# Second attention of a two-layer transformer kernel: VectorE instead of ScalarE copies the transposed probabilities out of PSUM bank 5

## The chip, the cores and the metric

The kernel runs on one core of a Trainium2 chip. The metric is the device time of one execution in microseconds; lower is better. Engines are named as in the profile: PE is TensorE (PEld its weight loads), DVE is VectorE, ACT is ScalarE, POOL is GpSimd, SP is SyncE, which issues most DMAs.

## The reference

The input x has 16 sequences of 128 tokens with 256 features, all in float32. Two blocks run one after the other, and x is added to the result.

- Block 1: a conditioned layer norm, self-attention with 16 heads of 128, an output projection, and a feed-forward network with 1024 hidden units and Gelu.
- Block 2: an RMS norm; queries for 16 heads and keys and values for 4 heads (each is shared by 4 query heads); RMS norm and rotary embedding of queries and keys; causal attention; an output projection; then a router that sends each token to 2 of 8 experts.

The part that matters here is the attention of block 2:

```python
q = rmsnorm(q, q_norm_w); k = rmsnorm(k, k_norm_w)      # then rotary embedding
k = jnp.repeat(k, n_rep, axis=1); v = jnp.repeat(v, n_rep, axis=1)
scores = jnp.einsum('bhqd,bhkd->bhqk', q, k) * scale
scores = jnp.where(causal[None, None], scores, jnp.finfo(scores.dtype).min)
attn = jnp.einsum('bhqk,bhkd->bhqd', jax.nn.softmax(scores, axis=-1), v)
hidden = hidden + attn @ o_w.T
```

## The kernel before, in words

The program is written by hand: each engine has its own instruction stream, in order, and waits on semaphores with fixed counts. No scheduler moves anything. The 16 sequences are handled in 4 groups of 4. The order of the stages is the first attention (to about 600 us), the first feed-forward network, the second attention (the stage of this change, about 650 to 1105 us), and the experts.

**The second attention** is a pipeline of steps. `attention2(step, expert)` calls an engine's `step(s)` for u = 0 to 15 in each group g = 0 to 3, and after the last group for u = 16 to 22: the drain, in which no new queries come in and from u = 19 on the first expert tiles are worked on too. One step brings in one key/value head of one sequence with its 4 query heads, so every tile is 128 x 512. `s.kv` is u mod 4. A step with kv = 0 also makes the keys and values of a new sequence (`new_seq`), one with kv = 1 scales and transposes the keys. `s.live(k)` is true where the work item that came in k steps ago is to be handled. An item goes through the steps like this:

- u: PE makes the queries in bank 0 (L1949). DVE multiplies them with the rotary tables into qr and rb (L1508, L1512), POOL adds the two (L642), ACT squares them into sq (L903), DVE sums that into q_ms (L1587), and POOL makes rq, the factor of the norm (L654, L658).
- u + 1: PE transposes qr into bank 4 (L2063), ACT copies it to q_t (L915).
- u + 2: PE makes mask and scores in bank 3 (L2093, L2096), once the exps of the item before have left the bank.
- u + 3: DVE takes the negative maximum nmax of bank 3 (L1550) and multiplies it to nb (L1554). ACT makes four exps into p2 (L889), each with a read of its accumulator. DVE makes rinv (L1576), POOL multiplies p2 by it (L646).
- u + 4: PE transposes p2 into bank 5 (L2071). **The copy of this change** takes bank 5 to the tile pt2 (L922 on ACT, shown in the profile as pt).
- u + 5: PE multiplies pt2 with the values into bank 6 (L2032), ACT rounds it into o2_hi (L910), DVE makes the remainder o2_lo (L1591).
- u + 6: PE multiplies both with the output weights into bank 7 (L2006), twelve matmuls. After the fourth head DVE adds bank 7 to xres (L1596), at kv = 1.

**The order within a step.** PE: keys, queries, output product (waits for o2_lo), values, weighted values (wait for pt2), transposes of qr and p2, keys' transposes, mask and scores (wait for the exps). At u = 12 the weighted values come before the values product, at u = 0 both products come before the keys. ACT: exps, key squares, sq, o2_hi, q_t, router logits (u = 11), **pt2**, v2 (kv = 0), k_t (kv = 1), weight pieces. DVE: nmax, nb, norm statistics (u = 7), key rotation, key scaling (kv = 1), query rotation, rinv, key and query sums, o2_lo, xres add (kv = 1), and then what only some steps have: norm_rows (L1032, u = 9), its transposed copies (L1040, u = 10), the routing parts (u = 11 to 14), placing of rows (`place_rows`, u = 15 and, for g of 2 and more, u = 0), the tables of the expert tiles (`first_tiles`, u = 16 and 18), and the remainders of weight pieces (L1639 for u = 5 to 12 of group 0, wd_lo in L1644 for u = 17 to 19), each after ACT has rounded its piece (L940, L948). POOL also scatters the token rows by indirect DMA (`send`, L614), the last eight at u = 16 to 18; SP loads the first expert tile when all of these have landed.

The semaphore that the copy counts up is g_ph. PE waits for it ahead of the weighted values and ahead of the next transposes into bank 5; the first expert tiles wait for its last count. g_tp counts the transposes, g_pvp the weighted values.

Of the kernel before, what the change touches and what calls it, by code (L numbers as in the profile page):

```python
# [24 lines left out]
ACT = mybir.ActivationFunctionType  # L25
# [28 lines left out]
def program(nc, ins, out):  # L54
    ctx = ExitStack()
    with ctx:
# [4 lines left out]
        def sb(name, shape, dtype=F32, at=None):  # L61
            size = 2 if dtype is BF16 else 4
            for n in shape[1:]:
                size *= n
            size = -(-size // 32) * 32
            if at is None:
                at = cursor[0]
                cursor[0] += size
            place[name] = (at, at + size)
            return nc.alloc_sbuf_tensor_at(name, shape, dtype, offset=at)  # L70

        def sem(name):
            return ctx.enter_context(nc.semaphore(name))
# [84 lines left out]
        pt2 = sb("pt2", [P, REP * T], at=W2 + 36 * KB)  # L158
# [77 lines left out]
        bank = [ctx.enter_context(nc.psum_tensor(f"bank{i}", [P, 512], F32)) for i in range(8)]  # L236
# [27 lines left out]
        def lo1(c, i):  # L264
# [23 lines left out]
        g_kp, g_vp, g_qp, g_tp, g_qtp, g_op, g_pvp, g_ktp, g_sp = (  # L288
            sem(f"g_{x}") for x in ("kp", "vp", "qp", "tp", "qtp", "op", "pvp", "ktp", "sp"))
        g_ex, g_ksq, g_sq, g_ph, g_vh, g_qt, g_oh, g_kt = (  # L290
            sem(f"g_{x}") for x in ("ex", "ksq", "sq", "ph", "vh", "qt", "oh", "kt"))
# [425 lines left out]
        def _(act):  # L717
            def logits_copy(r, src):

                act.wait_ge(t_lp, r + 1)  # L720
                if r == 0:
                    act.wait_ge(d_scratch, 48)
                nc.scalar.activation(lt[:], src[0:E, :], ACT.Copy).then_inc(t_lt, 1)
# [99 lines left out]
            n = NG * H  # L823
# [47 lines left out]
            def step(s):  # L871
                n, new_seq = s.n, s.new() and s.kv == 0
# [42 lines left out]
                    nc.scalar.activation(q_t[:, (s.u - 1) % 2], bank[4][:], ACT.Copy).then_inc(g_qt, 1)  # L915
                if s.u == 11 and not s.first:
                    logits_copy(s.g - 1, bank[2])
                if s.live(4):
                    act.wait_ge(g_tp, n - 3)
                    if s.had(5):  # L920
                        act.wait_ge(g_pvp, n - 4)
                    nc.scalar.activation(pt2[:], bank[5][:], ACT.Copy).then_inc(g_ph, 1)  # L922
                if new_seq:
                    act.wait_ge(g_vp, s.seq + 1)
                    if s.first and s.u == 0:
# [52 lines left out]
            def expert(i):  # L978
# [6 lines left out]
                if 0 <= i - 3 < NT:  # L985
                    expert_out(i - 3)

            attention2(step, expert)
            for i in range(len(DRAIN), NT + 3):
                expert(i)  # L990
# [7 lines left out]
        def _(dve):  # L998
# [20 lines left out]
            def norm_apply_rms(n, g):  # L1019

                dve.wait_ge(n_rs, n + 1)
                for b in range(GB):
                    last = nc.vector.tensor_scalar(xn[:, b], xres[:, bass.ds(g * GB + b, 1), :].rearrange("p a d -> p (a d)"),
                                                   rstd[:, b:b + 1], None, ALU.mult)
                last.then_inc(n_xn, 1)

            def norm_rows(n, g):

                dve.wait_ge(n_rs, n + 1)
                dve.wait_ge(d_router, 32)  # L1030
                for b in range(GB):
                    last = nc.vector.scalar_tensor_tensor(  # L1032
                        out=rows[:, b, 0:D], in0=xres[:, bass.ds(g * GB + b, 1), :].rearrange("p a d -> p (a d)"),
                        scalar=rstd[:, b:b + 1], in1=w_row[:], op0=ALU.mult, op1=ALU.mult)
                last.then_inc(n_xn, 1)
# [387 lines left out]
            n = NG * H  # L1423
# [93 lines left out]
            def step(s):  # L1517
                n, new_seq, prev = s.n, s.new() and s.kv == 0, 3 * NG + s.g - 1
# [73 lines left out]
                if s.kv == 1 and s.had(9):  # L1592

                    dve.wait_ge(g_op, 4 * (s.seq - 1))
                    xs = xres[:, bass.ds(s.seq - 2, 1), :].rearrange("p a d -> p (a d)")
                    nc.vector.tensor_tensor(xs, xs, bank[7][:, 0:D], ALU.add).then_inc(g_x, 1)  # L1596
                if s.u == 9:
                    if s.first:
                        norm_apply_rms(prev, done)
                    else:  # L1600
                        if s.g >= 2:
                            dve.wait_ge(d_send[0], 16 * 2 * GB * (s.g - 1))
                        norm_rows(prev, done)
# [85 lines left out]
            def expert(i):  # L1689
# [5 lines left out]
                if 0 <= i - 2 < NT:  # L1695
                    h_lo3(i - 2)

            attention2(step, expert)
            last_norm = 4 * NG - 1
            FETCHED = TC[0] + 7  # L1700
# [556 lines left out]
```

## Time and profile before

| | |
|---|---|
| median of 3 runs | 1239.65 us (1235.97 to 1241.87) |
| profiled execution, its own time | 1249.14 us |
| its span in the profile | 1247.4 us |
| granted TensorE clock over the span, mean | 0.975 |
| instructions | 22867 |

The profile shows one execution, and sums are made against its own time. The time outside the span is 1.7 us. Busy times count an engine's instructions from start to end; instructions of one engine can overlap a little, so that the next one starts before the one ahead has ended. "Idle before" is time in which an engine had nothing under way, with what ended it. The granted clock is a share of full speed.

### The profile page before, as it was taken

Reading aid. Unit: us, or ns where it says so; the run is one execution under the profiler, and the core shown is the slowest. Engines: PE = TensorE matmul, PEld = TensorE weight load, DVE = VectorE, ACT = ScalarE, POOL = GpSimd, SP = SyncE. Lnnn points to the kernel's source line nnn. Section 1 sums busy time; section 2 is a strip of 40 time slices with the busy share of each in tenths; the row PEclk is TensorE's granted clock in tenths of the full one; section 3 lists DMA queues with packets and bytes.
Section 4 is the critical chain, followed back from the end, with each engine's and each line's share of the span. In section 5 each row is a group of like instructions: output and inputs, shape, how many; then the busy total and the mean of one; then the engine's idle time right before and its main releaser. Section 6 shows DMA issues by size and latency. Waiting matters only on the chain.

```text
span 1247.4 us, 22867 instructions
## 1 busy us (share of the span) xinstructions
PE 1174.7 (94%) x7712; PEld 1040.9 (83%) x7744; DVE 742.7 (60%) x1619; ACT 657.4 (53%) x1866; POOL 522.6 (42%) x597
## 2 busy tenths in 40 slices
PE   6999999999999999989988999999999999878895
PEld 5888999999999999978876888888888887767795
DVE  3566554345434553367557776777777777756466
ACT  3454444444444434455435776666766666645453
POOL 4111131113111311143436766665876786733653
PEclk9999999999999999989998999999999999899898
DMA  9100000000000011041001029400000100224346
GB/s 339 57 1 1 18 1 18 1 1 1 18 1 1 1 41 45 3 183 35 18 18 51 1 71 306 126 1 1 23 14 2 60 18 6 64 70 142 119 127 198
DMA packets 46452, 68.78 MB, mean 55 GB/s; under 512 B 4741, under 2 KB 38537, under 8 KB 45355
## 3 DMA queue, kind: packets, MB, share of 16 engines
q1 hardware_dynamic: 42595, 58.89, 15.0%
q0 software_dynamic: 3744, 8.43, 1.9%
q8 instruction: 65, 1.06, 0.4%
q14 instruction: 48, 0.39, 0.1%
HBM read 41.17 MB, written 27.97 MB: 55 GB/s over the span
## 4 chain that ended last, share of the span: by engine, by line
PE 78%; POOL 3%; DVE 3%; issue 2%; DMA 2%; ACT 1%; another core or an unknown queue 0%; SPq 0%; POOLq 0%; DVEq 0%; ACTq 0%
PE bank L1761 12%; PE bank L1949 10%; PE bank L1798 9%; PE bank L2006 7%; PE bank L1829 6%; PE bank L2096 5%; PE bank L2032 4%; PE bank L1789 4%; PE bank L2137 4%; PE bank L1771 4%; PE bank L2168 2%; PE bank L2063 2%; PE bank L2071 2%; PE bank L1779 2%; PE bank L1890 2%
## 5 line engine op out<-in xcount | busy, mean ns | idle before, releaser
L568 POOL TENSOR_TENSOR p<-p,rinv 128x512 f32<-128x512 f32 x64 | 66.5, 1040 | 410.0 <-DVE rinv L1338 410.0
L889 ACT ACTIVATE p<-bank,nb,rq 128x128 f32<-128x128 f32 x256 | 113.7, 454 | 98.0 <-DVE nb L1554 98.0
L758 ACT ACTIVATE p<-bank,nmax 128x128 f32<-128x128 f32 x256 | 90.4, 366 | 117.1 <-DVE nmax L1326 117.1
L642 POOL TENSOR_TENSOR qr<-qr,rb 128x512 f32<-128x512 f32 x64 | 81.7, 1277 | 81.0 <-DVE rb L1512 79.6
L1761 PE MATMUL bank<-cur_hi,wqk_hi 128*128 128x512 f32 x256 | 108.8, 425 | 4.4 <-DVE cur_lo L1279 4.4
L1334 DVE COPY pt<-bank 128x512 f32<-128x512 f32 x64 | 44.2, 691 | 108.6 <-PE bank L1779 105.8
L1761 PE MATMUL bank<-cur_hi,wqk_lo 128*128 128x512 f32 x256 | 101.8, 398 | 0.0
L1761 PE MATMUL bank<-cur_lo,wqk_hi 128*128 128x512 f32 x256 | 101.7, 397 | 0.0
L767 ACT ACTIVATE o_hi<-bank,bqkv 128x512 fp32r<-128x512 f32 x64 | 44.1, 688 | 102.8 <-PE bank L1789 102.4
L1342 DVE SCALAR_TENSOR_TENSOR o_lo<-bank,bqkv,o_hi 128x512 fp32r<-128x512 f32 x64 | 48.0, 750 | 53.9 <-ACT o_hi L767 53.9
L1798 PE MATMUL bank<-wo_hi,o_hi 128*128 128x256 f32 x256 | 77.8, 304 | 0.4 <-DVE o_lo L1342 0.2
L1789 PEld LDWEIGHTS bank<-pt,v 128*128 128x128 f32 x512 | 67.2, 193 | 13.0 <-DVE pt L1334 8.5
L1829 PE MATMUL bank<-wv_hi,cur_hi 128*128 128x256 f32 x256 | 76.7, 300 | 0.0
L2006 PE MATMUL bank<-wo_hi,o_hi 128*128 128x256 f32 x256 | 74.7, 292 | 1.6 <-DVE o_lo L1591 1.6
L1789 PE MATMUL bank<-pt,v 128*128 128x128 f32 x512 | 68.8, 278 | 6.2 <-DVE pt L1334 6.2
L2006 PE MATMUL bank<-wo_hi,o_lo 128*128 128x256 f32 x256 | 73.7, 288 | 0.0
L2096 PE MATMUL bank<-k_t,q_t 128*128 128x128 f32 x512 | 69.4, 280 | 4.5 <-ACT p L889 2.7
L2006 PE MATMUL bank<-wo_lo,o_hi 128*128 128x256 f32 x256 | 73.5, 287 | 0.0
L1798 PE MATMUL bank<-wo_hi,o_lo 128*128 128x256 f32 x256 | 72.4, 283 | 0.0
L1798 PE MATMUL bank<-wo_lo,o_hi 128*128 128x256 f32 x256 | 72.3, 282 | 0.0
L2096 PEld LDWEIGHTS bank<-k_t,q_t 128*128 128x128 f32 x512 | 69.3, 196 | 2.6
L1829 PE MATMUL bank<-wv_lo,cur_hi 128*128 128x256 f32 x256 | 71.3, 278 | 0.0
(265 smaller groups left out, 3822.7 us busy)
## 6 DMA issues: line engine op xcount, KB each, us to landing
token_scratch<-empty SPq DMA_DIRECT2D x1, 13287.0 KB, 47.3
xs<-token_scratch SPq DMA_DIRECT2D x46, 129.0 KB
wqk_raw<-in_wqk SPq DMA_DIRECT2D x8, 512.0 KB, 10.3
gate<-gates_scratch SPq DMA_DIRECT2D x8, 512.0 KB
got_t<-expert_scratch SPq DMA_DIRECT2D x16, 256.0 KB, 3.4
w_raw<-in_w SPq DMA_DIRECT2D x2, 1408.0 KB, 6.0
xres<-in_x SPq DMA_DIRECT2D x4, 512.0 KB, 6.3
wv_raw<-in_wv SPq DMA_DIRECT2D x8, 256.0 KB, 10.3
```

Source lines behind the costliest of these rows:

```text
L568: nc.gpsimd.tensor_tensor(p1[:, h % 2], p1[:, h % 2], rinv[:, h % 2].unsqueeze(2).broadcast_to([P, GB, T]), ALU.mult).then_inc(a_pn, 1)
L642: nc.gpsimd.tensor_tensor(qr[:, s.u % 2], qr[:, s.u % 2], rb[:], ALU.add).then_inc(g_qr, 1)
L758: last = nc.scalar.activation(p1[:, h % 2, b], bank[3][:, b * T:(b + 1) * T], ACT.Exp, bias=nmax[:, h % 2, b:b + 1], accum_out=rsum[:, h % ...
L889: last = nc.scalar.activation(p2[:, (s.u - 3) % 2, j], bank[3][:, j * T:(j + 1) * T], ACT.Exp, scale=rq[:, (s.u - 3) % 4, j:j + 1], bias=n ...
L1761: last = pe.matmul(dst, l, r, start=(k == 0 and i == 0), stop=(k == KD - 1 and i == 2))
L1771: last = pe.matmul(bank[3][:, bs], q1[:, h % 2, bs], k1[:, h % 2, bs], start=True, stop=True)
L1789: last = pe.matmul(bank[5][:, bs], v1[:, h // 2 % 2, b, h % 2 * DH:h % 2 * DH + DH], pt1[:, bs], start=True, stop=True)
L1798: last = pe.matmul(bank[banks[b // 2]][:, b % 2 * D:b % 2 * D + D], l, r, start=(first and b % 2 == 0 and i == 0), stop=(last_one and i == 2),
L1829: last = pe.matmul(bank[2][:, j * 2 * DH:(j + 1) * 2 * DH], l, r, start=(k == 0 and i == 0), stop=(k == KD - 1 and i == 2))
L1949: last = pe.matmul(dst, l, r, start=(k == 0 and i == 0), stop=(k == KD - 1 and i == 2))
L2006: last = pe.matmul(bank[7][:, 0:D], l, r, start=(kv == 0 and j == 0 and i == 0), stop=(kv == HKV - 1 and j == REP - 1 and i == 2))
L2096: last = pe.matmul(bank[3][:, js], q_t[:, s.u % 2, js], k_t[:, slot, kv * T:(kv + 1) * T], start=False, stop=(j == REP - 1), skip_group_ch ...
```

## The change

The copy is taken out of ACT's step and put into DVE's, behind the xres add and ahead of what only some steps have. It waits for the same two semaphores and counts up the same one. Nothing else changes.

```diff
@@ -915,11 +915,6 @@
                     nc.scalar.activation(q_t[:, (s.u - 1) % 2], bank[4][:], ACT.Copy).then_inc(g_qt, 1)
                 if s.u == 11 and not s.first:
                     logits_copy(s.g - 1, bank[2])
-                if s.live(4):
-                    act.wait_ge(g_tp, n - 3)
-                    if s.had(5):
-                        act.wait_ge(g_pvp, n - 4)
-                    nc.scalar.activation(pt2[:], bank[5][:], ACT.Copy).then_inc(g_ph, 1)
                 if new_seq:
                     act.wait_ge(g_vp, s.seq + 1)
                     if s.first and s.u == 0:
@@ -1594,6 +1589,11 @@
                     dve.wait_ge(g_op, 4 * (s.seq - 1))
                     xs = xres[:, bass.ds(s.seq - 2, 1), :].rearrange("p a d -> p (a d)")
                     nc.vector.tensor_tensor(xs, xs, bank[7][:, 0:D], ALU.add).then_inc(g_x, 1)
+                if s.live(4):
+                    dve.wait_ge(g_tp, n - 3)
+                    if s.had(5):
+                        dve.wait_ge(g_pvp, n - 4)
+                    nc.vector.tensor_copy(pt2[:], bank[5][:]).then_inc(g_ph, 1)
                 if s.u == 9:
                     if s.first:
                         norm_apply_rms(prev, done)
```

## Rows read from the trace of the kernel before

**Rows 1.** The page, part 1: busy us (share of the span) xinstructions
```profile
PE 1174.7 (94%) x7712; PEld 1040.9 (83%) x7744; DVE 742.7 (60%) x1619; ACT 657.4 (53%) x1866; POOL 522.6 (42%) x597
```

**Rows 2.** By window: us, PE, PEld, DVE, ACT, POOL, PEclk, DMA share, GB/s
```profile
859.10:966.30 107.20, 106.78 (x672) 89.75 (x679) 79.59 (x176) 70.72 (x209) 76.27 (x89) 1.00 0.03 11
1074.00:1105.00 31.00, 18.07 (x91) 14.67 (x91) 18.26 (x38) 14.51 (x38) 16.81 (x15) 0.82 0.22 62
```

**Rows 3.** Groups by line: xcount | busy us, mean ns | idle before
```profile
L922 ACT ACTIVATE pt<-bank 128x512 f32<-128x512 f32 x64 | 39.1, 611 | 0.0
...
L1334 DVE COPY pt<-bank 128x512 f32<-128x512 f32 x64 | 44.2, 691 | 108.6 <-PE bank L1779 105.8
```

**Rows 4.** Who waited for whom on PE, 690 to 1090 us: total, times, longest
```profile
PE bank L2093 <- ACT p L889: 3.4, 1, 3.4
PE bank L2096 <- ACT p L889: 2.7, 1, 2.7
```

**Rows 5.** Order of time, DVE, then PE, plain steps: start us, us, what [idle before]
```profile
874.32 0.68 DVE L1550 TENSOR_REDUCE nmax<-bank 128x4 f32<-128x512 f32 x1
...
879.18 0.69 DVE L1550 TENSOR_REDUCE nmax<-bank 128x4 f32<-128x512 f32 x1 [0.21 <-PE bank L2096]
...
883.49 0.69 DVE L1591 TENSOR_TENSOR o_lo<-bank,o_hi 128x512 fp32r<-128x512 f32 x1 [0.24 <-ACT o_hi L910]
884.84 0.69 DVE L1550 TENSOR_REDUCE nmax<-bank 128x4 f32<-128x512 f32 x1 [0.66 <-PE bank L2096]
...
931.79 1.28 DVE L1040 COPY h_t<-bank 128x512 f32<-128x512 f32 x2
...
878.09 1.05 PE L2096 MATMUL bank<-k_t,q_t 128*128 128x128 f32 x8
...
883.75 1.05 PE L2096 MATMUL bank<-k_t,q_t 128*128 128x128 f32 x8
```

**Rows 6.** Order of time, DVE and ACT, steps 12 to 14 of group 2
```profile
945.74 0.69 DVE L1591 TENSOR_TENSOR o_lo<-bank,o_hi 128x512 fp32r<-128x512 f32 x1 [0.29 <-ACT o_hi L910]
...
948.49 0.69 DVE L1550 TENSOR_REDUCE nmax<-bank 128x4 f32<-128x512 f32 x1 [0.73 <-PE bank L2096]
...
954.99 0.68 DVE L1550 TENSOR_REDUCE nmax<-bank 128x4 f32<-128x512 f32 x1
...
960.82 0.68 DVE L1550 TENSOR_REDUCE nmax<-bank 128x4 f32<-128x512 f32 x1
...
947.43 0.59 ACT L922 ACTIVATE pt<-bank 128x512 f32<-128x512 f32 x1
```

**Rows 7.** Order of time, ACT, DVE and PE's loads, step 15 of group 2
```profile
963.47 0.21 ACT L889 ACTIVATION_READ_ACCUMULATOR p<-bank,nb,rq 128x1 f32 x1
...
964.80 0.68 DVE L1591 TENSOR_TENSOR o_lo<-bank,o_hi 128x512 fp32r<-128x512 f32 x1
...
964.51 0.10 PEld L2093 LDWEIGHTS bank<-mask,ident_b 128*128 128x128 bf16 x1
...
965.85 0.19 PEld L2006 LDWEIGHTS bank<-wo_hi,o_hi 128*128 128x128 f32 x1
```

**Rows 8.** The chain that ended last, and DVE's xres add, step 17 on
```profile
1088.27 0.48 ACT pt L922
...
1090.14 1.75 DVE wd_lo L1644
...
1097.47 3.82 DMA token_scratch<-rows,index
...
1104.42 0.69 PE bank L2117 x2
...
1088.91 0.41 DVE L1596 TENSOR_TENSOR xres<-xres,bank 128x256 f32<-128x256 f32 x1
```

**Rows 9.** POOL: its product of the first attention, and the last scatter
```profile
L568 POOL TENSOR_TENSOR p<-p,rinv 128x512 f32<-128x512 f32 x64 | 66.5, 1040 | 410.0 <-DVE rinv L1338 410.0
...
1097.47 2.15 POOL L614 DMA_INDIRECT token_scratch<-rows,index  x1 [0.30 <-issue]
```

## The prediction, made before the change was run

> **What bounds the kernel now.** I read the page first (busy shares), then the table by stage, then the groups of the copy, then who waited for whom on PE, and last the order of time inside the second attention. Over the whole span PE is busy 94%, VectorE (DVE) 60% and ScalarE (ACT) 53% [rows 1]. In one group of 16 steps of the second attention PE is busy 106.8 of 107.2 us at the full clock (granted 1.00, the 2.4 GHz level), DVE 79.6 and ACT 70.7 us [rows 2]. So this stage is bound by PE, and neither engine's load counts by itself. From 690 to 1090 us PE's matmuls are idle for exps (L889) at two places only, 3.4 and 2.7 us [rows 4], and both lie in the drain, the last steps without new queries, where PE is busy 18.1 of 31 us [rows 2]. There DVE and ACT in turn set the pace, and there a change of either shows.
>
> **What moves.** All 64 copies of bank 5 to pt2 leave ACT, where one is 0.61 us and 39.1 us in all [rows 3]. On DVE the same shape and source is 0.69 us in the first attention [rows 3]; two such copies out of a bank take 1.28 us together, so the next instruction starts 0.60 us after one [rows 5]. I take 0.60 (the cadence is what a chain pays), with 0.69 as the upper end. That makes 38 us more DVE work, 10 us per group of 16 steps: DVE goes to some 90 of 107 us and still fits. No DMA and no queue moves. What the new waits do is the question: the copy sits after o_lo (L1591) and the xres add, and ahead of the norm, routing and placing work of the step and of the next step's nmax (L1550). nmax leads to nb, the four exps, sq, q_ms, o_lo and the copy again. That loop is on DVE and ACT alternately, so a late nmax stays late until a step in which DVE would have waited for PE anyway.
>
> **Plain steps: nothing.** In the step that ends at 883.75 DVE starts o_lo at 883.49 and then idles 0.66 us for the scores before nmax at 884.84 [rows 5]. o_lo gives way at 884.09, the copy fills 0.60 to 884.69, nmax is not moved. With a backlog (nmax at 874.32 to nmax at 879.18, 0.21 idle) the loop needs 4.65 us, with the copy 5.25; PE's own step is 883.75 - 878.09 = 5.66 us [rows 5]. So a backlog shrinks by 0.4 us a step, and goes in the long steps that make keys and values. In the first group, DVE waited after o_lo for the w3 piece that ACT rounded behind its own copy; ACT is now 0.48 earlier with it and DVE uses the time for the copy: nothing. The cover in all these steps is DVE's wait for PE or ACT. Without it each step would pay 0.60.
>
> **Steps 12 to 15 of groups 1 to 3: 1.6 us each.** In step 12 PE makes the values product between the weighted values and the transposes. DVE is through with o_lo at 946.35 (945.74 plus its cadence), but the transposed probabilities are there at 947.43, when ACT took them [rows 6]. DVE works in order, so the router arithmetic behind the copy waits too: it starts at 948.03 and not at 946.35, 1.68 late. The 0.73 idle before nmax at 948.49 takes part of it: nmax of step 13 is 0.95 late. Step 13 adds 0.60 less a short idle ahead of o_lo, which I take as 0.2, step 14 adds 0.60; before the nmax of 954.99 and of 960.82 there is no idle [rows 6]. The nmax of step 15 is then about 1.95 late, and with it the exps and o_lo. The exps of step 15 end at 963.68 and PE loads for the mask at 964.51; o_lo ends at 965.48, and PE's load for the output product is at 965.85 [rows 7]. The first gives 965.63 against 964.51, 1.1 us of stall; the second 967.43 against 965.85, 1.6 us. These are one stall, not two: 1.6 us for each of groups 1 and 2. In groups 2 and 3, step 0 also ends with placing work, so the nmax of step 1 is 0.60 late at once; PE's slack for those exps is about as large, and I leave the tenth of a microsecond that may be missing to the range.
>
> **Drain: 2.3 us.** Group 3 brings its 1.95 into the drain. The copy of step 15 lies for the most part in DVE's wait for the rank matmuls, so I take 2.0 us at the nmax of step 16. The copy of step 16 adds 0.60, as DVE has no idle there up to the next nmax: 2.6. In step 17 the chain of before runs o_hi, pt (0.48 us on ACT), wd_hi, wd_lo, nmax [rows 8]. Here ACT's copy leaves the chain (wd_hi is ready 2.6 - 0.5 = 2.1 late), but DVE has o_lo, xres and its copy to do before wd_lo: the xres add starts at 1088.91 and takes 0.41, of which I count 0.35: 1088.91 + 0.35 + 2.6 + 0.60 = 1092.46 against 1090.14, 2.3 late [rows 8]. From there it goes through nmax, the exps, the POOL product, the last scatter at 1097.47 and the load of the first expert tile to PE at 1104.42 [rows 8]: 2.3 us, and the expert stage just starts later.
>
> **Sum.** 1.6 + 1.6 + 2.3 = 5.5 us. The profiled execution took 1249.14 us (span 1247.4), 9.5 above the median of 1239.65; it would become 1254.6, and the median 1245.2, +0.44%. A measurement of this kernel can tell about 0.5%, 6.2 us, from no change.
>
> **A rule weighed.** In the first attention, where DVE makes these copies at 0.69 us, POOL's product of the same shape takes 1.04 us [rows 3, 9]; I see no cost there. The last scatter of the drain took 2.15 us, beside DVE's wd_lo, whose inputs both lie in SBUF [rows 8, 9]. The Trainium skill, SBUF — State Buffer, Who interferes with whom, says that DVE and GpSimd share a port pair which one holds for a whole instruction, and that a copy can take it in its two-port form. VectorE: DVE Perf Modes, Why PSUM operands drop a tier, excludes that form for a PSUM source, as this one is. By the first sentence alone this would be a rival, the third below.
>
> **Rivals.**
> 1. *Hidden but for the drain, +2.3 us or less (1242).* It holds if DVE gets the copy in early enough in steps 12 to 15. For it: the plain steps. Against: the missing idle in rows 6. Chance 0.15.
> 2. *Slower: the copy costs 0.8 us, not 0.60, in the loop.* The 0.69 row plus a start after its waits of 0.1 would do. Each copy that is in a backlog chain then counts 0.2 more: four in each of groups 1 to 3 (2.4) and three in the drain (0.6), 3.0 more and 8.5 in all: 1248.2. The total passes 6.2 us at a cost of 0.65 us a copy: (6.2 - 5.5) / 15 = 0.05 more than mine. Chance 0.22.
> 3. *The copy holds POOL up.* Three copies of 0.69 before a product or scatter of the drain, 2.1 us more: 7.6, 1247.3. The trace bears it out for wd_lo, not for a copy out of a bank. Chance 0.05.
> 4. *Faster: ACT was the bound where PE waits.* ACT's 0.48 comes off each of steps 16 to 20 and DVE's copy is covered: 5 times 0.48 or 2.4 us, and PE's 6.1 us of waits for exps [rows 4] would be 3.7: 1237.3, and less if the steps before gain too (some waits of DVE for ACT's weight pieces). Against: only in step 17 is pt in the chain [rows 8]. Chance 0.06.
> That the code does not do what it says can be left out: 64 instructions go and 64 come.
>
> **The numbers.** My forecast gets 0.52. It spans 4.0 us (half a microsecond less at each of its three places) to 7.4 us (0.69 a copy, 15 times 0.09 or 1.4 more, and half a microsecond); three tenths of it lie above 6.2. Faster by over 0.5% (under 1233.4): 0.04, the better half of rival 4 and what scatter does. Slower by over 0.5%: 0.15 of the forecast, 0.22 and 0.03 of rivals 2 and 3, 0.40. Within 0.5%: the rest, 0.56. The range runs from the hidden case less 2 us of the scatter of three runs (1235.97 to 1241.87), 1240.0, to rival 2 plus somewhat more than that, 1251.0; under it lies rival 4 and a part of the scatter.
>
> **What would show it.** The 64 copies on DVE at 0.69 us, none on ACT; ACT near 60 and DVE near 90 us per group of 107. PE's waits for exps and o_lo in groups 1 and 2, about 1.5 us each, right at steps 14 to 0; a wait of DVE for the transposes of about 1 us in step 12; group 0 unchanged; the two drain waits longer by 2 and 0.6 us; PE's first expert tile some 5.5 us later against the start of group 1. If groups 1 and 2 last as long as before, the backlog argument is wrong; if every step is longer, the loop bounds the stage and I am far too low; if the drain is shorter, rival 4 holds.

## The result, and the profile of the changed kernel

| | kernel before | changed kernel |
|---|---|---|
| median, 12 runs each (those of the kernel before include its first three) | 1236.63 us (1233.48 to 1241.87) | 1243.81 us (1241.43 to 1249.18) |
| ratio, 95% interval | | 1.0053 (1.0039 to 1.0067) |
| profiled execution, span | 1249.14, 1247.4 us | 1249.18, 1247.4 us |

The change costs 0.53%, or 6.6 us (4.8 to 8.3). The medians alone differ by 7.2 us. One run of an experiment below (act1215, 1464.22 us at a granted clock of 0.75) was in a slow state and is in no ratio.

The two profiled spans are equal all the same. The difference lies behind this stage: from the first expert tile to the end the profiled execution of before took 143.0 us and that of after 136.0 us. Over all kernels here, none of which but the last three (wd) changes the work of that stretch, this part went from 133.5 to 144.4 us. It goes with the chip and not with the kernel: the four experiments on chip 1 took 133.5 to 136.1 us there, the eight on chips 3, 11 and 15 141.9 to 144.4 us, and the kernel before had medians of 1237.3 us on chip 1 and of 1244.7 and 1245.2 us on chips 11 and 15. The chips of the two profiles above are not on record, but 143.0 and 136.0 us look like one of each kind. So two spans tell nothing about a change of this size unless both come from one chip, and each experiment is compared with the kernel before on its own chip.

The stage itself repeats. I take the start of PE's load for the mask (L2093) in each step, counted from the one in step 9 of group 0, less the same in the kernel before. In the steps ahead of the edit in the kernels drain and wdbefore below, these marks agree with the kernel before to 0.03 us. ("S" is the start of the last scatter, "tile" PE's first expert tile.)

| late, us | g0 u11 | g1 u13 | g1 u15 | g2 u0 | g2 u15 | g3 u0 | g3 u13 | g3 u14 | g3 u15 | u16 | u17 | S | tile |
|---|---|---|---|---|---|---|---|---|---|---|---|---|---|
| after | 1.00 | 1.03 | 1.98 | 2.40 | 3.47 | 3.88 | 3.94 | 4.66 | 6.52 | 7.23 | 6.98 | 6.65 | 6.63 |

Group 0 brings 1.00, group 1 another 1.40 (2.40 - 1.00), group 2 1.48, group 3 up to step 16 3.35, and the drain gives 0.60 back: 6.63 at the tile, which is the measured 6.6.

The page of the changed kernel, part 1, answers to [rows 1]: DVE has 41.6 us more (784.3 against 742.7), ACT 31.6 less (its copies were 39.1 us long in all, but each overlapped its neighbours, so about 0.49 us of busy time goes with each), and PE the same work.

```profile
PE 1171.8 (94%) x7712; PEld 1038.0 (83%) x7744; DVE 784.3 (63%) x1683; ACT 625.8 (50%) x1802; POOL 519.4 (42%) x597
```

The window of 107.2 us at the same place as in [rows 2] (us, PE, PEld, DVE, ACT, POOL, PEclk, DMA share, GB/s), and from another view the copy (ns min/median/max). DVE is at 87, ACT at 61, PE 0.9 us less busy in the same time, at the full clock as before:

```profile
861.26:968.46 107.20, 105.84 (x656) 88.61 (x665) 86.67 (x190) 61.38 (x190) 74.67 (x87) 1.00 0.03 11
```

```profile
L1596 DVE COPY pt<-bank x64: 674/681/693, 679.3 to 1106.8; 128x512 f32<-128x512 f32 x64
```

Who waited for whom on PE from 690 to 1100 us (total, times, longest) answers to [rows 4]. The waits at L2093 were one of 3.4 us and are five of 6.9 us: four new places (step 11 of group 0 and step 15 of groups 1 to 3), the rest still the drain. The two waits of the drain are 3.1 and 3.0 us where they were 3.4 and 2.7.

```profile
PE bank L2093 <- ACT p L889: 6.9, 5, 3.1
PE bank L2096 <- ACT p L889: 3.7, 2, 3.0
PE bank L2006 <- DVE o_lo L1586: 0.9, 3, 0.3
```

Steps 12 to 15 of group 2 on DVE and then PE, in order of time, answer to [rows 6, 7]. In front of the copy DVE idles 0.95 us for the transposes. To compare times with the rows of before, add 2.79 us (0.34 for the start, 2.45 late). Then nmax is 0.82 late at 952.10 (948.49 before), 1.15 at 958.93 (954.99) and 1.74 at 965.35 (960.82), and there is no idle ahead of any of the three. At the end PE stands 0.59 us for the exps and 0.32 us for o_lo. By the marks, which also count what overlaps the end of the transposes, the two cost 1.02 and 0.41 us.

```profile
948.53 0.69 DVE L1586 TENSOR_TENSOR o_lo<-bank,o_hi 128x512 fp32r<-128x512 f32 x1 [0.29 <-ACT o_hi L910]
950.17 0.69 DVE L1596 COPY pt<-bank 128x512 f32<-128x512 f32 x1 [0.95 <-PE bank L2071]
...
952.10 0.68 DVE L1545 TENSOR_REDUCE nmax<-bank 128x4 f32<-128x512 f32 x1
...
958.93 0.68 DVE L1545 TENSOR_REDUCE nmax<-bank 128x4 f32<-128x512 f32 x1
...
965.35 0.68 DVE L1545 TENSOR_REDUCE nmax<-bank 128x4 f32<-128x512 f32 x1
...
968.35 0.38 PE L2093 MATMUL bank<-mask,ident_b 128*128 128x512 bf16 x1 [0.59 <-ACT p L889]
970.07 0.39 PE L2006 MATMUL bank<-wo_hi,o_hi 128*128 128x256 f32 x1 [0.32 <-DVE o_lo L1586]
```

Group 0 is not unchanged. DVE in steps 9 and 10 of the changed kernel, in order of time:

```profile
713.48 0.69 DVE L1596 COPY pt<-bank 128x512 f32<-128x512 f32 x1
714.08 1.13 DVE L1018 TENSOR_SCALAR xn<-xres,rstd 128x256 f32<-128x256 f32 x4
715.13 0.52 DVE L1639 TENSOR_TENSOR w_lo<-w_raw,w_hi 128x352 fp32r<-128x352 f32 x1
715.57 0.69 DVE L1545 TENSOR_REDUCE nmax<-bank 128x4 f32<-128x512 f32 x1
716.73 0.16 DVE L1549 TENSOR_TENSOR nb<-nmax,rq 128x4 f32<-128x4 f32 x1 [0.47 <-DVE nmax L1545]
...
720.51 0.68 DVE L1596 COPY pt<-bank 128x512 f32<-128x512 f32 x1
721.11 1.40 DVE L1040 TENSOR_SCALAR act_t<-bank,norm_w 128x512 f32<-128x512 f32 x2
722.42 0.52 DVE L1639 TENSOR_TENSOR w_lo<-w_raw,w_hi 128x352 fp32r<-128x352 f32 x1
722.86 0.69 DVE L1545 TENSOR_REDUCE nmax<-bank 128x4 f32<-128x512 f32 x1
```

The same in the kernel before (add 0.34 us to compare):

```profile
714.76 0.52 DVE L1639 TENSOR_TENSOR w_lo<-w_raw,w_hi 128x352 fp32r<-128x352 f32 x1
715.19 0.68 DVE L1550 TENSOR_REDUCE nmax<-bank 128x4 f32<-128x512 f32 x1
715.98 0.17 DVE L1554 TENSOR_TENSOR nb<-nmax,rq 128x4 f32<-128x4 f32 x1
...
719.77 1.40 DVE L1045 TENSOR_SCALAR act_t<-bank,norm_w 128x512 f32<-128x512 f32 x2
721.09 0.52 DVE L1639 TENSOR_TENSOR w_lo<-w_raw,w_hi 128x352 fp32r<-128x352 f32 x1
721.52 0.69 DVE L1550 TENSOR_REDUCE nmax<-bank 128x4 f32<-128x512 f32 x1
```

In step 9 the copy is covered: nmax is 0.04 late. But nb then stands 0.47 us after nmax (0.41 late). In step 10 the copy adds its whole 0.60, because act_t and w_lo follow each other with no idle: nmax is 1.00 late, and PE waits 1.0 us for the exps.

### The profile page after: what moved, and what is told of

Same layout as the page of the kernel before. It is cut to its first block, busy times and chain, and to the rows that moved or that the text cites. A ratio compares the mean times of both kernels' runs of the same rounds, so it can differ in the third digit from the quotient of the medians.

```text
span 1247.4 us, 22867 instructions
## 1 busy us (share of the span) xinstructions
PE 1171.8 (94%) x7712; PEld 1038.0 (83%) x7744; DVE 784.3 (63%) x1683; ACT 625.8 (50%) x1802; POOL 519.4 (42%) x597
## 3 DMA queue, kind: packets, MB, share of 16 engines
q8 instruction: 65, 1.06, 0.4%
## 4 chain that ended last, share of the span: by engine, by line
PE 75%; DVE 6%; issue 3%; POOL 3%; ACT 3%; DMA 2%; SPq 0%; POOLq 0%; DVEq 0%; ACTq 0%
PE bank L1761 12%; PE bank L1949 9%; PE bank L1798 9%; PE bank L2006 6%; PE bank L1829 6%; PE bank L1789 4%; PE bank L2096 4%; PE bank L2137 4%; PE bank L1771 4%; PE bank L2032 4%; PE bank L2168 3%; PE bank L1890 2%; PE bank L1779 2%; PE bank L2063 2%; PE bank L2071 2%
```

## The experiments

All kernels but the last group are the changed kernel with one edit, or mix the two engines: a helper `on_dve(s)` says in which steps DVE makes the copy, and ACT makes it in the others, at the place where it stood before. This is the edit for the first; the other mixtures differ in the returned line alone.

```diff
+        def on_dve(s):
+            return not (s.g >= 1 and 12 <= s.u < 16)
@@ ACT
+                if s.live(4) and not on_dve(s):
+                    act.wait_ge(g_tp, n - 3)
+                    if s.had(5):
+                        act.wait_ge(g_pvp, n - 4)
+                    nc.scalar.activation(pt2[:], bank[5][:], ACT.Copy).then_inc(g_ph, 1)
@@ DVE
-                if s.live(4):
+                if s.live(4) and on_dve(s):
```

The expectations of the first eight kernels count from step 2; the table counts from step 9, because in some kernels PE's marks of steps 2 to 8 of group 0 differed by up to 0.7 us, and they were level again by step 9.

| late, us | g0 u11 | g1 u13 | g1 u15 | g2 u0 | g2 u15 | g3 u0 | g3 u13 | g3 u14 | g3 u15 | u16 | u17 | S | tile |
|---|---|---|---|---|---|---|---|---|---|---|---|---|---|
| after | 1.00 | 1.03 | 1.98 | 2.40 | 3.47 | 3.88 | 3.94 | 4.66 | 6.52 | 7.23 | 6.98 | 6.65 | 6.63 |
| act1215 | 1.29 | 1.32 | 1.32 | 1.32 | 1.38 | 1.38 | 1.45 | 1.45 | 1.45 | 1.46 | 1.19 | 0.87 | 1.26 |
| g0only | 0.98 | 0.96 | 0.96 | 0.96 | 0.95 | 0.95 | 0.95 | 0.95 | 1.18 | 0.62 | 0.62 | 0.62 | 0.56 |
| step12 | 1.27 | 1.29 | 1.69 | 2.09 | 2.61 | 3.02 | 3.10 | 3.21 | 5.07 | 5.80 | 5.54 | 5.22 | 5.51 |
| actbusy | 1.53 | 1.63 | 2.59 | 3.00 | 4.08 | 4.49 | 4.57 | 5.29 | 7.16 | 7.89 | 8.09 | 8.13 | 8.63 |
| plain | -0.22 | -0.15 | -0.15 | -0.15 | -0.09 | -0.08 | -0.02 | -0.02 | -0.02 | 0.01 | 0.01 | -0.31 | -0.12 |
| w31late | 0.75 | 0.76 | 1.71 | 2.12 | 3.20 | 3.61 | 3.66 | 3.92 | 5.82 | 6.53 | 6.28 | 7.36 | 7.32 |
| atend | 2.06 | 2.23 | 2.63 | 3.03 | 3.64 | 4.04 | 4.18 | 4.22 | 5.25 | 5.26 | 5.56 | 5.68 | 5.52 |
| twice | 2.85 | 4.82 | 7.56 | 7.98 | 12.41 | 12.81 | 14.12 | 16.19 | 18.96 | 19.89 | 19.87 | 20.14 | 19.94 |
| drain | 0.00 | 0.00 | 0.00 | 0.00 | 0.00 | 0.00 | 0.00 | 0.00 | 0.00 | 0.03 | -0.23 | -0.54 | -0.16 |

**act1215: ACT copies in steps 12 to 15 of groups 1 to 3.**

> ACT makes the copies of steps 12 to 15 of groups 1 to 3, DVE the other 52. Theory of the missing idle: PE's extra time sits only where DVE is late into nmax with no idle to take it up. So the time from the mask of step 13 of group 1 to step 0 of group 2, now 1.41 us longer than before, and the same stretch a group on, 1.43, go back to within 0.1 of before; group 0 keeps its 1.0; the start of the drain loses the 2.6 that steps 14 and 15 of group 3 bring, and the drain keeps some 0.6 to 1. First expert tile 1.6 to 2.2 us later than before instead of 6.6. Rival, load: each DVE copy costs a 64th of 6.6 us, 0.10, wherever it is; 12 fewer give 5.4 us.

Measured 1239.46 us against 1237.32 for the kernel before, ratio 1.0021 (1.0005 to 1.0036). At the tile it is 1.26 late, under the 1.6 to 2.2 that I expected. The mark is 1.32 at step 13 of group 1 and 1.38 at step 0 of group 3: the stalls of groups 1 and 2 are gone, and group 3 with the drain adds nothing. So 5.4 of the 6.6 us come from the copies in twelve steps, and all that is left is group 0 (1.29 here, 0.98 in the next kernel, in which these steps have the same instructions). The 0.3 is there before step 9: DVE's xres add starts 1.07 us after the mark of step 9 here, 0.78 in g0only. Six kernels with the same instructions in group 0 lose 0.75 to 1.29 at step 11. That DVE's load by itself costs time (the rival) falls: DVE carries 52 of the 64 copies here.

**g0only: DVE copies in group 0 alone** (`s.g == 0 and s.u < 16`).

> DVE makes only the 12 copies of group 0 (steps 4 to 15), ACT the rest. Missing idle: all of it is in steps 10 and 11, 1.0 us, and nothing after it; the steps 0 of groups 1 to 3 and the first expert tile stay 1.0 later than before. Load: 12 times 0.10, 1.2 us, spread over steps 4 to 15. The two differ in the place: the step from mask to mask at 11 is 6.9 us and no other differs by over 0.1 from before, or every step is 0.1 longer.

Measured 1236.06 us in one run against 1237.32, which cannot tell 1 us; the marks can. All of group 0's loss comes at step 11, 0.98, and nothing is added up to step 14 of group 3. From step 15 on the marks move (1.18, then 0.62), and the tile is 0.56 late, not the 1.0 expected; I did not trace that.

**step12: in step 12 of groups 1 to 3 the copy stands behind the routing part.**

```diff
-                if s.live(4):
+                if s.live(4) and not (s.u == 12 and not s.first):
@@
                     routing_part(s.g - 1, s.u - 11)
+                if s.u == 12 and not s.first:
+                    dve.wait_ge(g_tp, n - 3)
+                    if s.had(5):
+                        dve.wait_ge(g_pvp, n - 4)
+                    nc.vector.tensor_copy(pt2[:], bank[5][:]).then_inc(g_ph, 1)
```

> The changed kernel, but in step 12 of groups 1 to 3 DVE makes the copy behind the routing part instead of ahead of it. If the wait for the transposes in front of the router arithmetic is what starts the lateness (0.95 us of 1.95 at nmax of step 15), the stall of groups 1 and 2 falls from 1.4 to about 0.5, group 3 and drain by about 0.9, in all some 2.8 us less of 6.6. If only the copy's own 0.6 counts and the wait does not, nothing changes (under 0.2 a group).

Groups 1 and 2 lost 0.82 and 0.93 us (from 1.27 to 2.09 and from 2.09 to 3.02) in place of 1.40 and 1.48; I had expected about 0.5. At the tile it is 1.1 us less than the changed kernel (5.51), not the 2.8 less that I had expected. The single run took 1236.60 us. The wait for the transposes in step 12 is real, but it is some 0.6 of a group's 1.4 us and not the greater part. The rest I put to the copies of steps 13 and 14, which have no idle to go into; no kernel takes those two out alone.

**actbusy: the changed kernel, and ACT still makes a copy of the same size** in the old place, into a tile that nobody reads. It reads a tile in SBUF and not bank 5, does not wait for the transposes, and takes 0.64 us.

```diff
+                if s.live(4):
+                    if s.had(5):
+                        act.wait_ge(g_junk, n - 4)
+                    nc.scalar.activation(junk[:], rope[:].rearrange("p c d -> p (c d)"), ACT.Copy).then_inc(g_junk, 1)
```

> The changed kernel, and ACT also makes a copy of a constant tile of the same size where its copy stood, so it is as busy as before. It tells what the relief of ACT gives back. Missing idle: ACT's relief helps where DVE waited for a weight piece (group 0) and in the last steps of the drain, so group 0 is longer by up to 0.6 a step that has a piece where DVE has no other idle (steps 9 to 12, together 0 to 1 us), the drain by 0 to 0.5; groups 1 and 2 stay at 1.4. Rival, relief gives nothing: 6.6 as it is, all stretches within 0.1.

Measured 1246.92 us in one run. At S it is 8.13 against 6.65, 1.48 more: 0.53 in group 0 (1.53 against 1.00), 0.13 up to step 16 (7.89 against 7.23 there), and 0.82 from step 16 on. Groups 1 and 2 add 1.47 and 1.49, nearly as before. So ACT's relief is worth nothing in the plain part, half a microsecond in group 0 and 0.8 us in the drain, which the changed kernel gets back.

**plain: ACT copies where it had cost something** (steps 9 and 10 of group 0, steps 12 to 15 of every group, step 16), DVE in the others: `not (s.g == 0 and 9 <= s.u <= 10) and not 12 <= s.u <= 16`.

> VectorE makes the copy only where the runs so far show that it costs nothing; ScalarE makes it in steps 9 and 10 of group 0, in steps 12 to 15 of every group and in step 16. Times of PE's mask load against the kernel before. Theory (a late nmax in the steps in which VectorE has no idle time is the whole cost): group 0 0.0 to 0.4 us late at step 11, groups 1 and 2 add 0.0, group 3 and the drain -0.3 to +0.3, the first expert tile 0.0 to 0.5 us late; the time is that of the kernel before, ratio 0.998 to 1.002. Rival, ScalarE's relief is worth something where nothing is late: the first expert tile comes 1 to 2 us earlier than before, as the kernel with ScalarE kept busy lost 1.9 us in the drain (ratio about 0.9985). Rival, mixing the copies of both engines costs more than either alone: over 1 us late.

Ratio 0.9997 (0.9981 to 1.0014), the tile 0.12 early. Forty-five of the copies on DVE cost nothing that can be measured, and none of them gains. (The 1.9 us that the expectation gives for the drain of actbusy mixes things: at the tile the whole difference is 2.00, with 0.53 of group 0 and 0.52 of the last scatter's landing in it. From step 16 to S it is 0.82.)

**w31late: the pieces of w3 for the second pass that POOL and ACT make in steps 13 to 16 one step later** (`W31_STEP = 14`).

> The changed kernel with POOL's and ScalarE's eight pieces of the second expert's w3 one step later (steps 14 to 17 in place of 13 to 16). The changed kernel came to step 15 of group 3 2.58 us later than it was at step 13, where groups 1 and 2 added 0.95 and 1.02. Theory (small VectorE operations with operands in SBUF are held until POOL's subtraction of a piece has ended): in step 13, now without pieces, nb takes 0.16 to 0.20 us again and not 0.62, the lateness at step 14 is some 0.45 us smaller than the 4.64 of the changed kernel; in steps 14 and 15 the operations beside the pieces are long again. Rival (the group is late because the router arithmetic is long by itself): 4.64 us at step 14 and 6.50 at step 15, and a long nb in step 13, as before.

This tested why group 3 gets 3.35 us late where groups 1 and 2 get 1.4. In the changed kernel, in order of time, DVE's small operations are four times as long as elsewhere, and each ends with POOL's subtractions (L674, two pieces a row):

```profile
1067.63 0.68 DVE L1545 TENSOR_REDUCE nmax<-bank 128x4 f32<-128x512 f32 x1
1068.41 0.62 DVE L1549 TENSOR_TENSOR nb<-nmax,rq 128x4 f32<-128x4 f32 x1
...
1073.85 0.92 DVE L1108 TENSOR_SCALAR r<-r 128x4 f32<-128x4 f32 x1
...
1075.02 0.67 DVE L1113 TENSOR_TENSOR comb<-probs,r 128x32 f32<-128x32 f32 x1
...
1067.17 1.85 POOL L674 TENSOR_TENSOR w_lo<-w_raw,w_hi 128x352 fp32r<-128x352 f32 x2
...
1073.80 1.83 POOL L674 TENSOR_TENSOR w_lo<-w_raw,w_hi 128x352 fp32r<-128x352 f32 x2
```

nb ends at 1069.03 and POOL's pair at 1069.02; comb at 1075.69 and 1075.63. In the kernel before, where DVE is through with them, r takes 0.17, comb 0.19 and nb 0.26. With the pieces one step later, in the same view:

```profile
1062.56 0.17 DVE L1549 TENSOR_TENSOR nb<-nmax,rq 128x4 f32<-128x4 f32 x1
...
1067.54 0.96 DVE L1108 TENSOR_SCALAR r<-r 128x4 f32<-128x4 f32 x1
...
1068.74 0.67 DVE L1113 TENSOR_TENSOR comb<-probs,r 128x32 f32<-128x32 f32 x1
```

nb is back at 0.17, and step 14 adds 0.26 us in place of 0.72, as the theory had it (0.45 less). In step 14, where pieces still stand, r and comb are still long and step 15 adds 1.90 as before (1.86). So 0.45 us (nb) of group 3's extra loss comes from a VectorE operation that slid under POOL's, shown by taking the piece away. For r and comb the durations say some 1.2 us more (0.92 - 0.17 and 0.67 - 0.19); no kernel takes their pieces away. The sum of 1.7 us fits: the nmax of step 15 is 3.37 us late here (1075.61 against 1067.96 + 0.34 + 3.94), against 1.74 us in group 2. The kernel as a whole is slower (7.32 at the tile, 1250.21 us in one run): two pieces now stand in step 17, and the first scatter of that step begins 1.95 us after POOL's product in place of 0.16.

**atend: the copy at the end of DVE's step.**

```diff
-                if s.live(4):
-                    dve.wait_ge(g_tp, n - 3)
...
                 if s.u == 9:
...
                                             ALU.subtract).then_inc(w_lo4, 1)
+                if s.live(4):
+                    dve.wait_ge(g_tp, n - 3)
...
```

> The copy at the end of VectorE's step, behind the norm, routing and placing work and the w3 piece of the step, and ahead of the next nmax. Theory (what costs is the added 0.60 us wherever nothing is idle, plus the wait for the transposes in step 12): group 0 late by about 1.2 us or more at step 11, since pt2 and with it the values product now also wait for the norm work of steps 9 and 10; groups 1 and 2 lose about as much as with the routing part alone ahead (0.80 and 0.88 us) or up to 1.4 us; first expert tile 4 to 7 us late. Rival (PE waits for pt2 once it comes late): PE's values product (its load of pt2) waits in the steps with much extra work, 1 us or more in each of steps 9, 10, 11 of every group, and the first expert tile is over 9 us late.

The tile is 5.52 late, better than the changed kernel by 1.1 us (1249.61 us in one run, against 1244.67 for the kernel before). Groups 1 and 2 lose 0.97 and 1.01, group 3 up to step 16 only 1.22, but group 0 costs 2.06, 1.05 of it in step 9. PE's waits for pt2 (the rival) are there, but not where the rival had them: 0.19 us in step 9 of group 0 and none in groups 1 and 2, then 0.9, 3.6 and 1.7 us from step 15 of group 3 on. They cost little: from step 16 to the tile it loses 0.26 us, where the changed kernel gets 0.60 back. A place for the copy that costs nothing in all steps is not among those tried.

**twice: DVE copies the bank two times in each step,** first into a tile that nobody reads.

```diff
                    if s.had(5):
                        dve.wait_ge(g_pvp, n - 4)
+                        dve.wait_ge(g_junk, n - 4)
+                    nc.vector.tensor_copy(junk[:], bank[5][:]).then_inc(g_junk, 1)
                    nc.vector.tensor_copy(pt2[:], bank[5][:]).then_inc(g_ph, 1)
```

> VectorE copies bank 5 twice, first into a tile that nobody reads, then into pt2: 0.60 us more in each of the 64 steps. Theory (a plain step has 0.4 to 0.66 us of room for one copy, the loop with two is 4.65 + 1.20 = 5.85 us against PE's 5.66): now the plain steps lose too, 0.1 to 0.25 us each, and the steps 12 to 15 of a group lose about 2.4 us more; a group is 4 to 6 us longer than before, the first expert tile 20 to 28 us late. Rival (the stage is held by PE alone in the plain steps, VectorE has slack left): plain steps as before, only steps 9 to 15 and the drain lose, 12 to 16 us in all.

1264.21 us in one run (1244.67 for the kernel before), the tile 19.94 late, just under the 20 to 28 of the theory and above the rival. Its plain steps in a row, nmax to nmax, DVE in order of time:

```profile
879.94 0.68 DVE L1547 TENSOR_REDUCE nmax<-bank 128x4 f32<-128x512 f32 x1
...
885.71 0.68 DVE L1547 TENSOR_REDUCE nmax<-bank 128x4 f32<-128x512 f32 x1
...
891.48 0.68 DVE L1547 TENSOR_REDUCE nmax<-bank 128x4 f32<-128x512 f32 x1
```

A loop of 5.77 us, against the 5.85 that the sum gave and PE's 5.66 [rows 5]. It loses 0.1 us a step, and the long steps mostly take that back: steps 3 to 12 of group 1 add nothing (4.90 to 4.82), those of groups 2 and 3 0.5 and 0.2. The loss is in steps 13 to 2 again, 4.15 us for the turn from group 1 to 2 (4.82 to 8.97 at step 2). The room for one copy in a plain step is real, and the second uses it up.

**drain: DVE copies in the drain alone** (`s.u >= 16`, four copies).

> VectorE makes the copy in the drain alone (steps 16 to 18); ScalarE makes the other copies. Theory (in the drain a copy costs its 0.60 us of VectorE's time in step 16, where no idle time is left, and is paid back in step 17, where ScalarE's copy was in the chain ahead of wd_hi): all marks up to step 16 as in the kernel before (0.0 to 0.1 us), the exps of step 17 some 0.6 us late, the first expert tile 0.0 to 0.6 us late. With the copy of step 16 left on ScalarE it was -0.12 at the tile. Rival (the lateness brought into the drain is a small part of its loss, the copies there are the loss): the first expert tile is 1.5 us late or more.

In one run (1242.12 us, 1244.97 for the kernel before) the last nmax and S are 0.55 early, not late: in the drain ACT's relief outweighs the copies by 0.54 us. How is told in the next part. The tile is only 0.16 early, as the last scatter took 4.17 us from its start to its landing, against 3.82 in the kernel before.

**The three pieces of wd in step 19** in place of 17, 18 and 19, where DVE has idle time (`late_chunk` gives the pieces 0, 1, 2 for u = 19 and none else): wd3 on plain, wdbefore on the kernel before, wdafter on the changed kernel.

```diff
-            c = u - (4 * GB + 1)
-            return None if not 0 <= c < 3 else slice(3 * c, min(3 * c + 3, E))
+            return {3: (0, 1, 2)}.get(u - 4 * GB, ())
@@ DVE (ACT likewise)
-                if late_chunk(s.u):
-                    tiles = late_chunk(s.u)
-                    dve.wait_ge(w_hi4, 2 * E + s.u - 4 * GB)
+                for c in late_chunk(s.u):
+                    tiles = slice(3 * c, min(3 * c + 3, E))
+                    dve.wait_ge(w_hi4, 2 * E + 1 + c)
```

> As the kernel with ScalarE's copy in steps 9, 10 of group 0 and 12 to 16 of each group and VectorE's elsewhere, and the three pieces of wd (wd_hi on ScalarE, wd_lo on VectorE) all in step 19, where VectorE has several us idle, not in steps 17, 18 and 19. Theory (in the drain wd_lo, 1.66 us of the chain ahead of the nmax of step 17, and the last scatter held until wd_lo has ended, 2.55 us in place of about 0.96, cost more than the copies ever did): nmax of step 17 comes 1.5 us earlier, the last scatter takes 0.96 to 1.2 us, the first expert tile comes 2.5 to 3.2 us earlier than in the kernel before, and the time falls by 1.5 to 3 us (ratio about 0.998). Rival (something else is late next, a transfer or the splits of step 19): the first expert tile is under 1 us earlier, or it is earlier but the work of step 19 makes the expert stage longer by as much, and the time is that of before.

> The kernel before with the three pieces of wd in step 19 alone. If the drain is held by wd_lo and not by which engine copies, this gains the same 2.5 to 3.2 us at the first expert tile as the mixed kernel does. If VectorE's copies are worth something in the drain (rival: pt in step 17 was the chain), the mixed kernel is ahead of this one by 0.5 us or more there.

> The changed kernel with the three pieces of wd in step 19 alone. The changed kernel is 7.23 us late at step 16 and 6.63 at the first expert tile. Theory (lateness of the change and the wd pieces are separate costs): still 7.2 late at step 16, some 4 to 5 at the first expert tile. The changed kernel already has its last scatter at 0.96 us, so it gains only the 1.7 us of wd_lo ahead of nmax and what the middle scatter of step 17 was held, less than the kernel before does. Rival (they hide in each other): no gain over 6.63.

| | ratio to before | S late | tile late | scatter, start to landing |
|---|---|---|---|---|
| wdbefore | 0.9983 (0.9967 to 0.9999) | -1.54 | -2.78 | 2.58 |
| wd3 | 0.9987 (0.9974 to 1.0001) | -1.19 | -1.06 | 3.79 |
| wdafter | one run, 1253.32 us against 1245.18 | 5.49 | 4.67 | 2.97 |

The kernel before with wd later has the lowest ratio of those run several times, 2.1 us less than before, with an interval that only just leaves out no change and overlaps that of wd3. It is 2.78 us early at the tile, as expected. wd3 is 1.06 us early and not the 2.5 to 3.2 that I expected, and its interval includes no change. wdafter is 7.29 late at step 16 and 4.67 at the tile, as expected: the lateness and the wd pieces are separate costs. In it wd_lo stands where DVE waited, and the last scatter instruction takes 0.96 us:

```profile
1095.45 4.56 DVE L1644 TENSOR_TENSOR wd_lo<-wd_raw,wd_hi 88x1536 fp32r<-88x1536 f32 x3 [1.16 <-ACT wd_hi L948]
...
1091.91 0.96 POOL L613 DMA_INDIRECT token_scratch<-rows,index  x1 [0.30 <-issue]
```

wd3 came into the drain 0.35 us later than wdbefore (a loss between steps 3 and 12 of group 3 that I did not trace) and is 0.35 later at S: between them, which engine copies makes no difference in the drain once wd_lo is out of it. Their 1.7 us at the tile are for the most part the landing (3.79 against 2.58, with POOL at 0.96 us in both), which is open.

## Why the prediction was right, and where it was not

The forecast was 5.5 us more; measured are 6.6 us, and 6.63 at the tile. In time that was 1245.2 forecast and 1243.81 measured, both against a median of before that came out 3 us lower over 12 runs than over the three shown. By the ratio, 0.53% lies on the bound of 0.5%, with an interval on both sides, where I had 0.56 for within and 0.40 for slower. The likeliest case was the right one, and the forecast mechanism (a late nmax, carried along DVE and ACT until DVE has idle time) is what the runs show. That the sum came within 1.1 us is in part luck, since errors of both signs stand in it. Term by term:

**Cost of a copy.** 0.68 us, and the next instruction 0.60 later (720.51 to 721.11): as taken. Rival 2 (0.8 us) falls. So does rival 3 (the copy holds POOL up): POOL's product of this stage (L646, 64 times) has a median of 1.04 us before and after, and none is over 1.05 us in the changed kernel.

**Plain steps: nothing.** Right. In act1215, 52 copies on DVE add nothing after step 11 of group 0 but 0.03 to 0.07 us at each turn to a new group, which stands for the tenth in step 1 that I had left to the range. The rest of the backlog argument (5.25 us against 5.66) is borne out by twice, with one term off: a loop with two copies is 5.77, not 5.85.

**Group 0: nothing. Wrong, 1.00 us.** The step that failed is the sentence that in the first group "DVE waited after o_lo for the w3 piece", with ACT 0.48 earlier to make up for the copy. That holds in step 9, where q_ms and o_lo do come 0.48 earlier (711.96 against 712.10 + 0.34) and nmax is only 0.04 late. In step 10, act_t and w_lo follow o_lo with no idle, so the 0.60 is added whole. I had looked at the w3 pieces as one pattern and had not read the two steps that also carry the norm. The other 0.41 is nb held in step 9, while POOL makes its constants. Over the 14 traces nb starts 0.46 to 0.48 us after nmax in the eight kernels whose nmax ends while one of POOL's two affine_selects runs, and 0.10 or 0.11 us after it in the six where it ends beside a memset or an iota. So it goes with what POOL does in that slot, but no kernel moves POOL's constants, and the cause is not shown.

**Groups 1 and 2: 1.6 us each; measured 1.40 and 1.48.** The mechanism and its place are right: the wait for the transposes in step 12 (0.95 us), nmax 0.82, 1.15 and 1.74 late where I had 0.95, 1.35 and 1.95, and two waits of PE at the end (0.59 and 0.32 us as the profile counts them, 1.43 by the marks, where I had 1.6 as one stall). The idle that takes some of it up was somewhat larger than I took. What I would have got wrong is the share of the two parts: step12 removes 0.6 and not 0.9.

**Group 3 and the drain: 2.3 us; measured 2.69 at the tile (6.63 - 3.94), by another sum.** I had 2.0 at nmax of step 16, then 2.6, then 2.3. Measured, less the 3.94 of step 13, they are 3.3, 3.0 and 2.7. The first was too small by 1.3 us. The term that was missing is the three small DVE operations that slid under POOL's w3 pieces (1.7 us by their durations).

The second step went the wrong way: I added 0.60 for the copy of step 16, and the lateness fell by 0.26, as it did in drain (0.03 at step 16, -0.23 at step 17). The copy does cost its 0.60 there, and DVE has no more idle than before (1.94 us for the exps and 0.31 for o_hi in both kernels). But two table operations behind it take 0.83 us less. In the kernel before, POOL waits 0.59 us for w_hi, which ACT makes behind its copy, and POOL's pieces then lie over count and passed:

```profile
1080.99 0.67 DVE L1173 TENSOR_TENSOR count<-count 128x8 f32<-128x8 f32 x1
1081.70 1.08 DVE L1175 TENSOR_TENSOR passed<-count,iota 128x217 f32<-128x217 f32 x1
...
1080.70 1.84 POOL L674 TENSOR_TENSOR w_lo<-w_raw,w_hi 128x352 fp32r<-128x352 f32 x2 [0.59 <-ACT w_hi L945]
```

In the changed kernel POOL begins at once and is through at 1089.67, before passed starts:

```profile
1089.16 0.53 DVE L1168 TENSOR_TENSOR count<-count 128x8 f32<-128x8 f32 x1
1089.73 0.39 DVE L1170 TENSOR_TENSOR passed<-count,iota 128x217 f32<-128x217 f32 x1
...
1087.79 1.88 POOL L674 TENSOR_TENSOR w_lo<-w_raw,w_hi 128x352 fp32r<-128x352 f32 x2
```

The operation passed takes 0.39 us in drain too, where nothing but the last four copies is changed, and 1.08 in plain, where ACT makes the copy of step 16. So the term that I left out is again DVE held under POOL, this time with the other sign. The third, 0.3 back because ACT's copy leaves the chain while DVE has o_lo, xres and copy to do before wd_lo, is right: wd_lo is 6.67 late (1097.15 in the order of time, against 1090.14 + 0.34) and o_lo ahead of it 6.97 (1095.61 against 1088.30 + 0.34). The chain of the changed kernel, start us, us, what, shows it (a step of the chain starts where the one ahead ends, so wd_lo stands at 1097.23); wd_lo no longer waits for wd_hi, as it did for 0.82 us:

```profile
1095.09 0.50 ACT o_hi L910
1095.65 0.57 issue
1096.22 0.41 DVE xres L1591
1096.63 0.60 DVE pt L1596
1097.23 1.66 DVE wd_lo L1644
1098.89 0.61 DVE nmax L1545
...
1104.46 3.75 DMA token_scratch<-rows,index
...
1111.39 0.69 PE bank L2117 x2
```

So of two errors, 1.3 us too little and 0.9 too much, 0.4 us is left, the 0.3 us too much in groups 1 and 2 takes most of that back, and what is left of the whole error is the 1.0 us of group 0. My sign that PE's two waits of the drain would grow by 2 and 0.6 us did not come true (3.1 against 3.4, and 3.0 against 2.7): I put that to PE itself coming late into the drain, having stood 1.68 us for the exps in step 15. Rival 4 (ACT was the bound) had a part of the truth: ACT's relief in the drain is worth 0.8 us by actbusy, and in drain it outweighs the copies by 0.5. It is smaller than what the late nmax brings in.

**The rule weighed.** I had looked at the two engines' sharing only for the new copy against POOL, and there it costs nothing. What it costs is indirect: the copy moves DVE's other operations in time. The rows of r, comb and nb under L674 show operations with both ends in SBUF that end with POOL's, while nmax at 1067.63, a reduction whose source is a bank, kept its 0.68 us beside the same POOL operations (whether for the bank or as a reduction, no run tells). The Trainium skill, SBUF — State Buffer, Who interferes with whom, says that a DVE instruction with two SBUF inputs contends with a GpSimd instruction that reads SBUF, that the one that starts first keeps the shared ports to its end, and that a `tensor_scalar` can take them as well. The trace agrees: nb, comb, count and passed have two SBUF inputs, r is a `tensor_scalar`, and POOL reads both of its inputs from SBUF.

## What to carry to other kernels

An engine at 80 of 107 us has room on average and may have none in the steps that matter: read, for each kind of step, whether there is idle time between the added operation and the next one that another engine waits for, and do it for every step with work of its own (here 9 and 10 of group 0, 12 to 15, 16), not for one of each pattern. Where a lateness is carried, list what runs on the other engines in the new time slots, too: 0.2 us operations can become 0.9 us ones there. Measure a change of this size by marks inside the stage, since marks in unchanged steps repeated to 0.03 us while the span of one execution hid the whole difference. And compare times on one chip only: the kernel before had medians 8 us apart in the measurements on two chips.

## What the runs showed of the hardware beyond what I had expected

- Four-column VectorE operations in SBUF took 0.62 and 0.92 us (nb, r) in place of 0.17 us when POOL subtracted 128 x 352 tiles in SBUF, and ended with POOL's. It holds for a `tensor_scalar` with one tensor input (r<-r) too. A 217-column one (passed) took 1.08 in place of 0.39.
- The landing of the last scatter, counted from its start, goes only in part with how long POOL holds it. Held for 2.5 us (five kernels) it landed after 4.03 to 4.27 us, held for 2.0 to 2.15 us (four) after 3.62 to 3.82, and held for 0.96 to 1.10 us (five) after 2.58 to 3.79. The kernel before (2.15 and 3.82) and the changed one (0.96 and 3.75) alone would hide that. Why the shortest hold has landings 1.2 us apart is open.
- The stretch from the first expert tile to the end took 133.5 to 136.1 us on chip 1 and 141.9 to 144.4 us on chips 3, 11 and 15. The mean granted clock there (0.92 in the profile of before with 143.0 us, 0.93 in that of after with 136.0, 0.92 in one of chip 1 with 133.5) does not explain it; what differs between the chips is open.
